# Sixteen-head attention: query and key projections and the output mix issued in the scores' 64x64 tiles

## The reference, cut to what matters

```python
x = layernorm(features)                       # context, 1601 rows
lat = layernorm(latents)                      # the stream, 2048 rows
q = (lat @ Wq) * 64 ** -0.5                   # 16 heads of 64
kv = concat(x, lat)
k, v = kv @ Wk, kv @ Wv
out = softmax(q @ k.T) @ v                    # for each head
return out @ Wo                               # gated and added to the stream
```

## Time and profile before

| | |
|---|---|
| median of three runs | 3096.9 us (3095.3 to 3097.13) |
| span of the profiled execution | 3090.4 us |
| PE busy | 2900.9 us (94%) |
| DVE busy | 2226.4 us (72%) |
| ACT busy | 1946.4 us (63%) |
| POOL busy | 514.4 us (17%) |

### The profile page before, as it was taken

The page is one execution under the profiler, slowest core; times in us unless marked ns, Lnnn a source line. Parts: engine busy times, 40 slices in busy tenths (PEclk is TensorE's granted clock), DMA queues, the critical chain, the costliest instruction groups (busy, mean ns, idle before and its releaser), DMA issues. The chain is left out here.

```text
span 3090.4 us, 71594 instructions
## 1 busy us (share of the span) xinstructions
PE 2900.9 (94%) x29558; PEld 1442.7 (47%) x29558; DVE 2226.4 (72%) x2813; ACT 1946.4 (63%) x2654; POOL 514.4 (17%) x573
## 2 busy tenths in 40 slices
PE   5999999999999999999999969999997998989989
PEld 3444444444444444444444536322223666557665
DVE  6888888888888888888878875200004887768876
ACT  5665665656656656656556633799995776347752
POOL 0000000000001001000000010200001774337720
PEclk8999999999999999999999979999998999999999
DMA  2000000000000000000000011211111000100000
GB/s 81 9 2 7 3 2 7 3 2 9 2 7 4 2 7 3 2 2 17 2 2 2 2 51 35 77 36 28 28 28 54 12 11 10 52 14 18 4 1 28
DMA packets 30221, 51.70 MB, mean 17 GB/s; under 512 B 6223, under 2 KB 22722, under 8 KB 28738
## 3 DMA queue, kind: packets, MB, share of 16 engines
q1 hardware_dynamic: 29890, 46.92, 4.9%
HBM read 41.04 MB, written 5.83 MB: 15 GB/s over the span
## 5 line engine op out<-in xcount | busy, mean ns | idle before, releaser
L815 ACT ACTIVATE a_probs<-PS 128x1024 f32<-128x1024 f32 x928 | 950.1, 1025 | 571.8 <-PE PS L568 560.5
L581 PE MATMUL PS<-a_probs,a_V 64*64 64x512 f32 x7424 | 984.9, 590 | 5.8 <-DVE a_heads_outT L1007 3.6
L1067 DVE TENSOR_TENSOR a_prob_sums<-a_prob_sums,a_probs 128x1024 f32<-128x1024 f32 x512 | 628.3, 1227 | 110.1 <-ACT a_probs L815 85.6
L1064 DVE SCALAR_TENSOR_TENSOR a_prob_sums<-a_probs,a_valid,a_prob_sums 128x1024 f32<-128x1024 f32 x384 | 508.4, 1324 | 74.9 <-ACT a_probs L815 60.9
L568 PE MATMUL PS<-a_Q_hi,a_K_hi 64*64 64x512 f16 x3712 | 389.8, 381 | 5.8 <-ACT a_probs L815 4.9
L568 PE MATMUL PS<-a_Q_hi,a_K_lo 64*64 64x512 f16 x3712 | 386.4, 377 | 2.6 <-issue 2.6
L568 PE MATMUL PS<-a_Q_lo,a_K_hi 64*64 64x512 f16 x3712 | 386.5, 378 | 0.0
L581 PEld LDWEIGHTS PS<-a_probs,a_V 64*64 64x64 f32 x7424 | 293.6, 133 | 166.4 <-issue 21.2
L2125 ACT ACTIVATE c_cT<-PS 128x1024 f32<-128x1024 f32 (+1 forms) x312 | 303.3, 1082 | 1.6 <-PE PS L2064 0.8
L67 POOL CAST a_heads_hi<-a_heads_outT 128x512 f16<-128x512 f32 x31 | 49.6, 1600 | 1441.9 <-DVE a_heads_outT L1023 1441.9
L568 PEld LDWEIGHTS PS<-a_Q_hi,a_K_hi 64*64 64x64 f16 x3712 | 119.9, 106 | 260.7 <-issue 254.9
(11 more groups left out here) (371 smaller groups left out, 4621.1 us busy)
## 6 DMA issues: line engine op xcount, KB each, us to landing
c_Qop<-q_part SPq DMA_DIRECT2D x96, 64.0 KB, 2.2
c_Kop<-k_part SPq DMA_DIRECT2D x96, 50.0 KB, 2.0
d_raw<-in_l1f_w_dram SPq DMA_DIRECT2D x18, 256.0 KB, 3.1
d_tables<-in_rotary_dram SPq DMA_DIRECT2D x2, 2048.0 KB, 10.8
X<-in_x_dram SPq DMA_DIRECT2D x2, 1024.0 KB, 9.5
out_dram<-X SPq DMA_DIRECT2D x8, 256.0 KB, 2.1
c_cT<-in_ctxT_dram SPq DMA_DIRECT2D x1, 1601.0 KB, 9.2
a_probs<-in_ctx_dram SPq DMA_DIRECT2D x3, 512.0 KB, 5.0
```

What stands on the lines that cost most here:

```text
L581: last = nc.tensor.matmul(m.PS[64 * h:64 * h + 64, PVB + g, :], V[e][rows, s, 64 * h:64 * h + 64], probs[n % 4][rows, h * BANK:(h + 1) * B ...
L815: nc.scalar.activation(probs[n % 4][:], m.PS[:, b0:b0 + 2, :].rearrange("p b c -> p (b c)"), ACT.Exp).then_inc(exped, 1)
L1064: nc.vector.scalar_tensor_tensor(out=sums, in0=new, scalar=valid[:, s:s + 1], in1=sums, op0=ALU.mult, op1=ALU.add).then_inc(summed, 1)
L1067: nc.vector.tensor_tensor(sums, sums, new, ALU.add).then_inc(summed, 1)
```

## The change

Query and key units and mixes are issued in 64x64 tiles, like the scores. Two units go together: the quarter of the array that takes the upper 64 rows of the contraction writes unit u[0] in bank UNIT while the lower 64 rows write u[1] in bank TOTAL (phase 0, at step n); at step n + 1 the halves are exchanged and both accumulations end (phase 1). Keys are cut in 8 units of 464 columns. Values stay in full tiles. The squared lengths (`norm`) move beside the totals, to the same steps, and write bank UNIT; the turn moves from step 82 to 97. The tables move: units at 28, 40, 46, 52, 58 and 70, 75, 80, 85 instead of eleven places; mixes at 12, 16, 20, 24; totals at 36, 66, 92. ACT and DVE take row units three steps after phase 0, values two after. One function, `both_free`, holds all waits for the two banks.

```diff
-        MIX_AT = {12: (0, 1), 15: (2, 3), 18: (4, 5), 21: (6, 7)}
-
-        UNIT_AT = {28: (2, 3), 39: (4,), 44: (5, 6), 57: (7, 8), 67: (9,), 72: (10, 11), 78: (12,), 82: (13,),
-                   86: (14, 15), 95: (16, 17), 100: (18, 19)}
+        MIX_AT = {12: (0, 1), 16: (2, 3), 20: (4, 5), 24: (6, 7)}
+
+        ROWS_AT = {28: (2, 3), 40: (4, 5), 46: (6, 7), 52: (8, 9), 58: (10, 11)}
+        VALUES_AT = {70: (12, 13), 75: (14, 15), 80: (16, 17), 85: (18, 19)}
+        UNIT_AT = {**ROWS_AT, **VALUES_AT}
+
+        TAKEN_AT = {**{n + 3: units for n, units in ROWS_AT.items()}, **{n + 2: units for n, units in VALUES_AT.items()}}
+        SQUARED_AT = {n + 5: units for n, units in ROWS_AT.items()}
+        ADDED_AT = {n + 3: units for n, units in MIX_AT.items()}
 
         EARLY, EARLY_AT = (0, 1), 12
-        NORM_AT = {39: 0, 67: 1, 78: 2}
-        TURN_AT = 82
+        TURN_AT = 97
 
         SPLIT_AT, FIRST_SPLIT_AT = 104, 2
-        LATE_TOTAL_AT, TOTAL_AT = 3, {33: 0, 62: 1, 91: 2}
+        LATE_TOTAL_AT, TOTAL_AT = 3, {36: 0, 66: 1, 92: 2}
+        NORM_AT = TOTAL_AT
...
+        KUNIT = KEYS // NKU
+        kcols = [(u * KUNIT, KUNIT) for u in range(NKU)]
...
+                def project_rows(i, us, phase):
+
+                    if phase == 1:
+                        hold(unit_halved, (i - 1) * len(ROWS_AT) + (us[0] - len(EARLY)) // 2 + 1)
+                    products = [(w_lo, kv_hi), (w_hi, kv_lo), (w_hi, kv_hi)]
+                    for j, (w, kv) in enumerate(products):
+                        for k in range(DK):
+                            for c in range(2):
+                                for r in range(2):
+                                    rows, cols, at = slice(64 * r, 64 * r + 64), slice(64 * c, 64 * c + 64), (r + phase) % 2
+                                    u, bank = us[at], (UNIT, TOTAL)[at]
+                                    c0, n = unit_columns(u)
+                                    c0 += 0 if u < NKU else LAT0
+                                    last = nc.tensor.matmul(m.PS[cols, bank, 0:n], w[1 if u < NKU else 0][rows, k, cols],
+                                                            kv[rows, k, c0:c0 + n], start=(phase == 0 and j + k == 0),
+                                                            stop=(phase == 1 and j + k == DK + 1))
+                    if phase == 0:
+                        last.then_inc(unit_halved, 1)
+                    else:
+                        last.then_inc(projected, 2)
...
                 def norm(i, g, e):
 
                     pe.wait_ge(squared, i * NORMS + 4 * (g + 1))
                     for j in range(4):
-                        u = 4 * g + j
-                        n = kcols[u][1] if u < NKU else BANK
-                        for r in range(BANK // n):
-                            last = nc.tensor.matmul(m.PS[32 * j:32 * j + 32, TOTAL, r * n:(r + 1) * n], head_ones[:],
-                                                    squares[(3 * e + g) % 2][j][:, 0:n], start=True, stop=True,
-                                                    tile_position=(0, 32 * j))
+                        n = unit_columns(4 * g + j)[1]
+                        last = nc.tensor.matmul(m.PS[32 * j:32 * j + 32, UNIT, 0:n], head_ones[:],
+                                                squares[(3 * e + g) % 2][j][:, 0:n], start=True, stop=True,
+                                                tile_position=(0, 32 * j))
...
+                def mix_rows(i, us, phase):
+
+                    if phase == 0:
+                        if us[0] == 0:
+                            pe.wait_ge(wo_split, i + 1)
+                        else:
+                            pe.wait_ge(added, i * MIXES + us[0])
+                        pe.wait_ge(heads_split, i * CHUNKS + us[0] // 2 + 1)
+                    else:
+                        hold(mix_halved, i * len(MIX_AT) + us[0] // 2 + 1)
+                    for t in range(2):
+                        for j, (heads, w) in enumerate([(heads_lo, wo_hi), (heads_hi, wo_lo), (heads_hi, wo_hi)]):
+                            for c in range(2):
+                                for r in range(2):
+                                    rows, at = slice(64 * r, 64 * r + 64), (r + phase) % 2
+                                    u, bank = us[at], (UNIT, TOTAL)[at]
+                                    t0 = (2 * u + t) * P + 64 * c
+                                    last = nc.tensor.matmul(m.PS[64 * c:64 * c + 64, bank, t * D:(t + 1) * D],
+                                                            heads[rows, t0:t0 + 64], w[rows, :],
+                                                            start=(phase == 0 and t == 0 and j == 0),
+                                                            stop=(phase == 1 and j == 2), skip_group_check=True)
+                    if phase == 0:
+                        last.then_inc(mix_halved, 1)
+                    else:
+                        last.then_inc(mixed, 2)
...
+                def both_free(i, n):
+
+                    pe.wait_ge(added, i * MIXES)
+                    pe.wait_ge(unit_free, (i + 1) * UNITS + units_before(n))
+                    pe.wait_ge(peaked, (i + 1) * 3 + norms_before(n))
+                    pe.wait_ge(inverted, (i * CHUNKS + totals_before(n)) * PARTS)
+                    if n > TURN_AT:
+                        pe.wait_ge(bounded, i + 2)
...
-                        if n in MIX_AT and not first:
-                            for u, bank in zip(MIX_AT[n], (UNIT, TOTAL)):
-                                if u > 1:
-                                    pe.wait_ge(added, (i - 1) * MIXES + u - 1)
-                                mix(i - 1, u, bank)
-                        for u, bank in zip(units_at(i, n), (UNIT, TOTAL)):
-                            if u not in EARLY:
-                                pe.wait_ge(unit_free, (i + 1) * UNITS + units_before(n))
-                                pe.wait_ge(added, i * MIXES)
-                            if bank == TOTAL and n > min(TOTAL_AT):
-                                pe.wait_ge(inverted, (i * CHUNKS + totals_before(n)) * PARTS)
-                                pe.wait_ge(peaked, (i + 1) * 3 + norms_before(n))
-                                if n > TURN_AT:
-                                    pe.wait_ge(bounded, i + 2)
-                            project(i + 1, u, bank)
-                        if n in NORM_AT and not last_pair:
-                            pe.wait_ge(unit_free, (i + 1) * UNITS + units_before(n))
-                            pe.wait_ge(peaked, (i + 1) * 3 + NORM_AT[n])
-                            pe.wait_ge(inverted, (i * CHUNKS + totals_before(n)) * PARTS)
-                            norm(i + 1, NORM_AT[n], 1 - e)
+                        for phase in range(2):
+                            if n - phase in MIX_AT and not first:
+                                mix_rows(i - 1, MIX_AT[n - phase], phase)
+                            if n - phase in ROWS_AT and not last_pair:
+                                if phase == 0:
+                                    both_free(i, n)
+                                project_rows(i + 1, ROWS_AT[n - phase], phase)
+                        if n == EARLY_AT and first:
+                            for u, bank in zip(EARLY, (UNIT, TOTAL)):
+                                project(i + 1, u, bank)
+                        if n in VALUES_AT and not last_pair:
+                            both_free(i, n)
+                            for u, bank in zip(VALUES_AT[n], (UNIT, TOTAL)):
+                                project(i + 1, u, bank)
+                        if n in TOTAL_AT:
+                            if not last_pair:
+                                both_free(i, n)
+                                norm(i + 1, NORM_AT[n], 1 - e)
+                            pe.wait_ge(added, i * MIXES)
+                            total(i, TOTAL_AT[n])
                         if n == TURN_AT and not last_pair:
```

More of the change, by code:

```diff
@@ L369, in context_attention, with taken_at, squared_at @@
         LAST_MIX_BANKS = (0, 1, 2, 3, UNIT, PVB, PVB + 1, TOTAL)
-        def units_at(i, n):
-            if n == EARLY_AT and i == 0:
-                return EARLY
-            return UNIT_AT.get(n, ()) if i + 1 < PAIRS else ()
+        def taken_at(i, n):
+            if n == EARLY_AT + 2 and i == 0:
+                return EARLY
+            return TAKEN_AT.get(n, ()) if i + 1 < PAIRS else ()
+        def squared_at(i, n):
+            if n == EARLY_AT + 4 and i == 0:
+                return EARLY
+            return SQUARED_AT.get(n, ()) if i + 1 < PAIRS else ()
         def units_before(n):
@@ L393, in context_attention @@
         held = m.sem("a_held")
+        unit_halved, mix_halved = m.sem("a_unit_halved"), m.sem("a_mix_halved")
         widened = m.sem("a_widened")
@@ L403, in context_attention @@
         MAX_SCORED, MAX_REDUCED = ST * len(spans) + 1, ST * len(spans) + 2
```

(31 more changed lines are left out.)

6 lines of the change are left out of this document (3 added, 3 removed).

## The result

The changed kernel takes 3117.0 us (median of 4 runs, 3114.9 to 3121.2), the kernel before 3097.0 in the same comparison: ratio 1.0069, 95% interval [1.0057, 1.0081]. The forecast was 3112 with a range of 3101 to 3123. The change makes the kernel slower by about 0.7%, as forecast; the sum lacked 5 us.

What follows compares the result with a forecast made beforehand. PE was taken to bound the 16-head attention. Chunk waits of 34.9 us less 19.7 us saved gave +15.2: profiled span 3105.6, plus 6.5 to the median, 3112 us; range 3101 to 3123.

Steps and rivals of the forecast that it cites:

- The chunk waits: Applies at steps 29, 58 and 87 wait for DVE's head addition, no longer hidden by visits: 4.99 us a pair, 34.9 us.
- Step 58: Chunk end with no visit before its apply; ACT's squares make the next exponential 0.28 us late: 2.24 us lost.
- Step 29: Chunk end where phase one of units 2 and 3 covers 1.17 of 1.96 us: 0.79 us lost.
- The saving: Fewer changes of tile shape on PE, 0.235 us a visit and 0.115 an inner change: 2.81 us a pair, 19.7 us.
- change of shape within a visit: Second change of tile shape inside one PE visit, read at step 39: 0.115 us, four a pair saved.
- Rivals 3 and 4: 3: mix and key groups in small tiles start too slowly, 3153 us, 6%; 4: each phase costs entry and exit, 3142, 3%.
- Rival 3's floors: Small matmuls' start-to-start floors: about 25 ns, adding nothing, or about 62 ns with hardware decode off, about 3177 us.
- The added waits on the first phases: Waits before phase one of units and mixes: counted as nothing, at most 0.1 us for each of 9 visits, 6 us.
- DVE's pile at the totals: DVE work after a total, 5.0 us, delays accumulation some 4.4 us; buffers forgive about 4.9; if not, 10 us.

Runs made afterwards that it cites:

- 1: Kernel before, only units 7 and 8 moved from step 57 to 58 and units 14 and 15 from 86 to 85: 3122.4 us, ratio 1.0085.
- 2: Changed kernel, visit of units 10 and 11 moved from step 58 to 57, that of units 18 and 19 from 85 to 86: 3092.8 us, ratio 0.9996.
- 3: Changed kernel, DVE's take_heads issued ahead of accumulate: 3099.5 us, ratio 1.0016 to the kernel before.
- 6: Changed kernel with visits at 57 and 86, take_heads ahead of accumulate, and mixes, key and query units in full tiles: 3096.8 us, ratio 1.0014.
- 7: Changed kernel with visits at 57 and 86, take_heads ahead of accumulate, and squared lengths one step ahead of the totals: 3085.4 us, ratio 0.9974.
- 9: Changed kernel, only its five waits at a pair's end moved to step 110: 3109.3 us, ratio 1.0047 to the kernel before.
- 8: Changed kernel with visits at 57 and 86, take_heads ahead of accumulate, and the five end waits at step 110: 3070.2 us, ratio 0.9926.
- 11: Kernel before, with the five waits of both_free at a pair's end in place of its one: 3088.2 us, ratio 0.9982.
- 12: Kernel before, with nine waits at a pair's end in place of its one: 3096.2 us, ratio 1.0007.

## Why the prediction was right, and where a term was missing

- **The chunk waits** (predicted 34.9 us, 4.99 a pair): the step that decides, and it holds. Measured from the timelines are 0.87 + 1.96 + 1.96 = 4.79 a pair, 33.5 us. Shown from both sides: uncovering the ends in the kernel before gives the loss without the change (1), covering them takes it out of the change (2), and shortening the chain takes out the share that the prediction gave for it (3).
- **Step 58** was mis-sized: the 0.28 us for ACT's squares did not come. The exponential behind the apply starts 0.21 us after it (two in 2.08 us from 397.01), as in pair 7 (0.23); ACT had made good its delay a step before. Step 29 cost 0.87 against 0.79 (in two of the pairs about as forecast).
- **The saving** (19.7 us): the mix visit shows it at its place, 1.30 against 1.53. In the whole, 6 gives 17.6 us for the small tiles' 14.8, and 7 gives 5.3 for the 4.9 of three entries and exits. By its own row the change of shape within a visit is 0.107 us rather than 0.115 (1.85 - 1.293 - 0.235 - 0.215), 0.2 us in all. Rivals 3 and 4 are out: groups of 256 columns start 0.11 apart, and no phase has a gap at its entry.
- **Rival 3's floors and the change of shape.** The groups of four in 0.11 us are 27 ns a matmul on average. This agrees with the lower of the two floors that the Trainium skill gives on its page "TensorE: Matmul & The Clock Gate", section "Wait — 56ns, not 53.3ns?" (about 25 ns), and rules out the upper one (about 62 ns) for this program. The 0.235 us that a change of shape costs fit what the page "TensorEngine Tiling (Array Packing)" of the Trainium skill, section "Key Properties", says in words, that changing the tiling mode drains the engine; it gives no figure, and no run here shows that a drain is what takes the time.
- **The added waits on the first phases**, counted at nothing: nothing at steps 24 and 29. The 3.0 us at L661 are one gap of 0.4 to 1.0 us in the first mix of each of pairs 1 to 5. It stands inside the first phase, after 17, 14, 12, 9 and 7 of its 24 matmuls, so it is not the waits at its entry. What it is stays open.
- **DVE's pile at the totals**, forgiven: PE's wait for the exponentials stayed (4.9 us and 4.5, 12 times each), and taking the pile apart gained nothing (7).
- **The missing term**: the prediction worked out a visit's waits only where something arrives late, and gave those of `both_free(i, STEPS)`, long satisfied, no price. At the pair's end they stand ahead of a branch with 2.4 us of cover; the idle time at the first matmul rose from 8.1 to 15.3 us, and moving the five waits brings it back to 8.1 (9) and 8.2 (8). What these waits cost hangs on the rest of the program, as 11 shows, and how is open.

The bill: 33.5 - 19.7 + 7.2 = 21.0 us. In the profiles ACT's first exponential starts at 74.8 and its last at 1771.1 us before, and at 76.2 and 1793.3 after: the attention grew by 20.8 us. The bill takes the saving as it was forecast. With the smaller rows (the clock 0.7 us more by the estimate, the other waits about 1 less) the saving that the profiles leave is between 19 and 20 us, which bears it out within those 2 us. The other 3.0 us of the span's 23.8 lie ahead of the attention (1.5) and behind it (1.5), where the program did not change; in the experiments the first exponential started between 74.2 and 80.4. The spans differ by more than the medians (20.0): in every run that has both, the span is about 1.8 us under the time, so the profiled execution of the kernel before took about 3092 us, 5 under its median, and the one after is 1 under its own. So the nearness of forecast and result rests on the chunk ends and the saving; the missing term was small beside the range.

## What to carry to other kernels

A visit at the place where a buffer changes hands is cover, and its cost there is partly nothing; before moving work by a step, ask which wait it hid. Here moving two visits by one step cost 23 us (2) while the rewriting of the work gained some 20. Waits that are long satisfied are worth trying some steps ahead of a branch: in the changed kernel that took 7 us of idle time off, and at their new place they cost nothing that was seen. In the kernel before there was nothing to gain. And when two kernels differ by a few us, look at the granted clock of their profiles before naming a cause.

## What the runs showed of the hardware

- PE's compare-and-branch at the start of a pair takes 3.3 to 5.1 us here, and the engine only has the matmuls already queued to fill it. The page "Advanced Engine Details and Errata" of the Trainium skill, section "Control Flow Timing", gives about 108 ns for a compare-and-branch. One of PE's in each trace comes near that (0.08 us, at 1955.8 us of the kernel before); the others differ by a factor of 30 and more, also one of the same source line as the short one (L2099, 3.27 us at 2342.7). What the time is spent on no run here shows.
- Waits that are already satisfied are not always free on PE's queue just ahead of such a branch: five cost 7 us of idle time in one program (changed against 9) and nothing in another (11).
- At an idle stretch of PE at a pair's start the granted clock can fall to 0.50 for 3.4 or 6.8 us, with score groups 0.43 us apart instead of 0.215. It was so at 3.69 us (pair 7 of the changed kernel) and at 2.23 and 2.02 us in 12, but not at 2.49 us (pair 7) in 8, nor at 1.64 us (pair 3) of the changed kernel.
- Matmuls of 256 columns in 64x64 tiles start 27 ns apart on average (four in 0.11 us), with the weight load of each.
